# A graph network on one core: the event tiles of layer 1 made as one-hots on VectorE and multiplied in the fifth section, not loaded as byte rows in the last one

## What is computed

```python
def _L1_gnn_ref(x, edge_index, Ws, bs, ln_w, ln_b):
    deg = jnp.zeros((n,), x.dtype).at[dst].add(1.0) + 1.0
    dinv = jax.lax.rsqrt(deg)
    enorm = (dinv[src] * dinv[dst])[:, None]
    self_norm = (dinv * dinv)[:, None]
    h = x
    for l in range(Ws.shape[0]):
        hw = h @ Ws[l]
        agg = jnp.zeros_like(hw).at[dst].add(enorm * hw[src])
        agg = agg + self_norm * hw + bs[l]
        mean = jnp.mean(agg)
        var = jnp.mean(jnp.square(agg - mean))
        hn = ln_w[l] * (agg - mean) * jax.lax.rsqrt(var + EPS) + ln_b[l]
        h = jax.nn.relu(hn)
    return h
```

## Time and profile before

| | us |
|---|---|
| median of 3 runs | 13834.2 |
| lowest and highest | 13832.89, 13850.3 |
| profiled execution, device time | 13845.09 |
| its span, first to last instruction | 13843.3 |
| mean TensorE clock granted, of full speed | 0.697 |

### The profile page before, as it was taken

The page is one execution under the profiler, slowest core; times in us unless marked ns, Lnnn a source line. Parts: engine busy times, 40 slices in busy tenths (PEclk is TensorE's granted clock), DMA queues, the critical chain, the costliest instruction groups (busy, mean ns, idle before and its releaser), DMA issues. The chain is left out here.

```text
span 13843.3 us, 151624 instructions
## 1 busy us (share of the span) xinstructions
PE 7164.9 (52%) x44130; PEld 5810.4 (42%) x44130; DVE 7167.8 (52%) x18509; ACT 4855.9 (35%) x7954; POOL 5410.8 (39%) x5426
## 2 busy tenths in 40 slices
PE   2333333325555555550053000036399999999788
PEld 2222222214454444440032000035255788888676
DVE  5556555634444444442042000158378777777666
ACT  0000000003333333330042000014288777777566
POOL 4555555555555555555714777720300000000111
PEclk6555555556666666665576555568699999999899
DMA  3334333423222222227185000039366888888798
GB/s 125 121 121 133 127 121 120 137 80 66 64 65 63 64 65 63 65 57 40 29 219 147 20 20 20 3 84 223 76 204 204 240 272 254 274 253 271 158 186 173
DMA packets 2774800, 1739.57 MB, mean 126 GB/s; under 512 B 1804710, under 2 KB 2613388, under 8 KB 2773940
## 3 DMA queue, kind: packets, MB, share of 16 engines
q1 hardware_dynamic: 2434740, 1298.35, 36.7%
q10 hardware_dynamic: 165920, 277.72, 5.6%
q0 software_dynamic: 173408, 154.46, 5.0%
HBM read 1065.70 MB, written 506.69 MB: 114 GB/s over the span
## 5 line engine op out<-in xcount | busy, mean ns | idle before, releaser
L838 POOL DMA_INDIRECT records<-RT,IDX x1664 | 1620.3, 974 | 1470.2 <-ACT RT L1598 972.1
L808 POOL DMA_INDIRECT G<-node_table,IDX x1664 | 1605.3, 965 | 1351.7 <-issue 1286.0
L882 POOL DMA_INDIRECT adj<-OH,EA x1664 | 1720.2, 1034 | 639.3 <-issue 639.3
L1276 PE MATMUL PS<-ring_f,terms_r 128*128 128x448 f32 x8232 | 1725.0, 369 | 34.3 <-DVE ring_f L2525 24.9
L1276 PEld LDWEIGHTS PS<-ring_f,terms_r 128*128 128x128 f32 x8232 | 1531.7, 188 | 216.7 <-DVE ring_f L2525 68.5
L2525 DVE CAST ring_f<-raw_f 128x1792 fp32r<-128x1792 uint8 x1323 | 1409.3, 1092 | 395.3 <-DMA raw_f<-adj 245.2
L1762 ACT CAST ring_f<-raw_f 128x1792 fp32r<-128x1792 uint8 x882 | 1465.5, 1691 | 418.4 <-DMA raw_f<-adj 260.3
L1052 PE MATMUL PS<-OH 128*98 128x128 bf16 x3328 | 453.5, 317 | 1806.9 <-remote 855.4
L1052 PEld LDWEIGHTS PS<-OH 128*98 128x98 bf16 x3328 | 365.8, 199 | 1973.4 <-remote 884.3
L2037 DVE TENSOR_TENSOR_SCAN S<-M,S,PS 128x512 f32<-128x512 bf16 x621 | 791.8, 1275 | 748.8 <-issue 517.1
L2030 DVE TENSOR_SCALAR OH<-iota_b,AG 128x128 bf16<-128x128 bf16 (+1 forms) x4480 | 836.0, 269 | 567.5 <-issue 290.6
(11 more groups left out here) (404 smaller groups left out, 14295.4 us busy)
## 6 DMA issues: line engine op xcount, KB each, us to landing
raw_f<-adj SPq DMA_DIRECT2D x2205, 224.0 KB
adj<-Z ACTq DMA_DIRECT2D x105, 1568.0 KB
AG<-adj SPq DMA_DIRECT2D x735, 224.0 KB
G<-records SPq DMA_DIRECT2D x624, 128.0 KB
M<-same_dst SPq DMA_DIRECT2D x416, 128.0 KB
fill_rows<-Z ACTq DMA_DIRECT2D x104, 512.0 KB
runs_l<-R SPq DMA_DIRECT2D x208, 256.0 KB
G<-fill_rows SPq DMA_DIRECT2D x208, 256.0 KB
```

Source lines behind the costliest of these rows:

```text
L808: pool.indirect_dma_start(G[:, i, q * D:(q + 1) * D], None, table, bass.IndirectOffsetOnAxis(ap=IDX[:, i, q:q + 1], axis=0)).then_inc(sem( ...
L838: pool.indirect_dma_start(rec, bass.IndirectOffsetOnAxis(ap=IDX[:, i, q:q + 1], axis=0), RT[:, i, q, :], None).then_inc(sem(f"scattered{i} ...
L882: pool.indirect_dma_start(adj_cells, bass.IndirectOffsetOnAxis(ap=CELL[:, at:at + 1], axis=0), VAL[:, at:at + 1], None).then_inc(sem(f"cel ...
L1276: m = pe.matmul(half_of(x, h)[:, c, :], stat, RINGF[q % NR][:, h * QW + c * HW:h * QW + (c + 1) * HW], start=K == 0, stop=False, skip_grou ...
```

## The change

- The last section no longer has the event tiles: it has 2 row tiles instead of 9, and the ring of layer 1 turns over 686 tiles instead of 735. Four spare tiles fill the last round: they are loaded and turned, PE only counts them.
- `rows_of` keeps the event's destination in `vrow`, less one where there is no event. DVE writes, ahead of the first tile, 98 columns of `dsj` (= `below`), which is `vrow` less 128 times the tile's number.
- In the fifth section (`VPART` = 4, 8 row tiles) DVE makes for each group 7 tiles of one-hots (`virtual_ones`): `iota_f` compared with `dsj`, 128x1792, written as bf16 in two buffers by turns (`VOH`). PE multiplies these seven ahead of the group's eight byte tiles.
- `VIRT_AT` is now the round before the fifth section, and the additions on DVE are placed by tile (`LAST_OF[u] + NR`), no longer by round.
- POOL issues 25 blocks before `virtual_rows` and 14 after it, where it was 35 (after the first 13) and 4.

```diff
-        PART = [list(range(CUTS[c], CUTS[c + 1])) + (list(range(NJ, AB)) if c == NCK - 1 else []) for c in range(NCK)]
+        PART = [list(range(CUTS[c], CUTS[c + 1])) for c in range(NCK)]
+        VPART = 4
...
-        VIRT_AT = LAST_OF[NJ // (2 * GT) * (NCK - 1) - 1] // NR
+        VIRT_AT = LAST_OF[NJ // (2 * GT) * VPART - 1] // NR
+        VOH = [r.bitcast(BF16) for r in REST]
...
+        ONCE = -(-UR * NJ // NR) * NR
+        SPARE = list(range(UR * NJ, ONCE))
...
-            adj_out(NB // 4, NB - 4)
+            adj_out(NB // 4, NB - 14)
             pool.wait_ge(*dve_at("srow_ready"))
             virtual_rows(0, VT)
-            adj_out(NB - 4, NB)
+            adj_out(NB - 14, NB)
...
+                    if c == VPART:
+                        if g == 0:
+                            pe.wait_ge(sem("virt_ready"), 1)
+                        for k in range(NV):
+                            pe.wait_ge(sem("v_ready"), NG2 + g * NV + k + 1)
+                            products(lambda t: VT3[:, t, k * D:(k + 1) * D], VOH[(g * NV + k) % 2], base, x, k == 0, False).then_inc(sem("fm_t"), 1)
...
+            def virtual_ones(g):
+
+                if g:
+                    then(dve.tensor_scalar(dsj, dsj, float(-2 * QW), None, ALU.add))
+                for k in range(NV):
+                    n = g * NV + k
+                    if n >= 2:
+                        dve.wait_ge(sem("fm_t"), NG2 + n - 1)
+                    dve.tensor_tensor(VOH[n % 2].rearrange("p (j c) -> p j c", c=P), rowbc(iota_f[:, :], 2 * GT),
+                                      bc(dsj[:, k * 2 * GT:(k + 1) * 2 * GT], [P, 2 * GT, P]), ALU.is_equal).then_inc(sem("v_ready"), 1)
...
                 for i in BY_DVE:
+                    n = r * NR + i
+                    before = n - (NR - BY_DVE[-1] + BY_DVE[0] if i == BY_DVE[0] else 2)
+                    for u, (c, g) in enumerate(UNIT):
+                        if before < LAST_OF[u] + NR <= n:
+                            if c < NCK - 1:
+                                add_part(u)
+                            else:
+                                scaled(0, g)
+                        if c == VPART and before < FIRST_OF[u] <= n:
+                            virtual_ones(g)
...
-            AFTER = {(LAST_OF[u] + NR) // NR: u for u in range(len(UNIT) - 1)}
-            assert len(AFTER) == len(UNIT) - 1
-            for r in range(NG2 * NK):
+            for k in range(NV):
+                for j in range(2 * GT):
+                    t = dve.tensor_scalar(dsj[:, k * 2 * GT + j:k * 2 * GT + j + 1], vrow[:, k:k + 1], float(-j * P), None, ALU.add)
+            then(t)
+            for r in range(ONCE // NR):
                 if r == VIRT_AT:
                     virtual_terms(0)
                 to_bf16_first(r)
```

More of the change, by code:

```diff
@@ L263, in gnn_kernel @@
         ON_ACT = [K < NJ and n % 2 == 0 for n, (_, K) in enumerate(TILE)]
-        RE = UE * AB
+        ONCE = -(-UR * NJ // NR) * NR
+        SPARE = list(range(UR * NJ, ONCE))
+        RE = ONCE + (UE - UR) * AB
         NW = 7
@@ L417, in gnn_kernel @@
         srj = below[:, 0:NV * 2 * GT]
+        dsj = srj
         assert MID_AT[5] + HALF <= EA_AT + 3 * SLOT and EA_AT + 3 * SLOT + HALF <= EA_END
@@ L727, in _ @@
                         group_end(g, g, g % 2)
+            for n in SPARE:
+                i, r = n % NR, n // NR
+                if i in BY_ACT:
+                    sp.wait_ge(sem("conv_a"), r * NA + i // 2 + 1)
+                else:
+                    sp.wait_ge(sem("conv_d"), r * ND + i // 2 + 1)
+                sp.dma_start(RAW[i], adj[0:P, 0:2 * QW]).then_inc(sem(f"ring_in{i}"), 16)
             sp.wait_ge(sem("conv_a"), A_BASE)
@@ L1334, in by_parts @@
                             pe.wait_ge(sem("conv_d"), r * ND + ND + i // 2 + 1)
[L1335 to L1338, removed]
+                        products(lambda t: TERMS[t][:, K * D:(K + 1) * D], RING[i], base, x, c != VPART and K == CUTS[c],
+                                 c < NCK - 1 and K == PART[c][-1]).then_inc(sem("ring_free"), 1)
                         n += 1
@@ L1341, in by_parts @@
                         own(g, x)
+                pe.wait_ge(sem("group_done"), NG2)
+                for n in SPARE:
+                    i, r = n % NR, n // NR
+                    if i in BY_ACT:
+                        pe.wait_ge(sem("conv_a"), r * NA + NA + i // 2 + 1)
+                    else:
+                        pe.wait_ge(sem("conv_d"), r * ND + ND + i // 2 + 1)
+                    pe.sem_inc(sem("ring_free"), 1)
             projected(0)
@@ L1752, in _ @@
             virtual_terms(0)
-            with act.Fori(VIRT_AT, NG2 * NK) as r:
+            with act.Fori(VIRT_AT, ONCE // NR) as r:
                 to_bf16(0, r)
@@ L2300, in rows_of @@
                 then(dve.tensor_copy(cols[:, :], vrow[:, :]))
+                then(dve.scalar_tensor_tensor(vrow[:, :], row_f[:, :], 0.0, vrow[:, :], ALU.min, ALU.add))
                 dve.sem_inc(sem("dve_at"), 1)
@@ L2406, in to_bf16 @@
                     dve.tensor_copy(RING[i], RAW[i]).then_inc(sem("conv_d"), 1)
+            def virtual_ones(g):
[7 more added lines that the diff above has]
+                                      bc(dsj[:, k * 2 * GT:(k + 1) * 2 * GT], [P, 2 * GT, P]), ALU.is_equal).then_inc(sem("v_ready"), 1)
+            FIRST_OF = [LAST_OF[u] + 1 - len(PART[c]) for u, (c, _) in enumerate(UNIT)]
             def to_bf16_first(r):
                 for i in BY_DVE:
+                    n = r * NR + i
[4 more added lines that the diff above has]
+                                add_part(u)
+                            else:
+                                scaled(0, g)
+                        if c == VPART and before < FIRST_OF[u] <= n:
+                            virtual_ones(g)
                     dve.wait_ge(sem(f"ring_in{i}"), r * 16 + 16)
@@ L2509, in _ @@
                 to_bf16_first(r)
[L2510 to L2514, removed]
             statistics(0, scaled(0, NG2 - 1))
```

4 lines of the change are left out of this document (2 added, 2 removed).

## The result

| | us |
|---|---|
| median of 4 runs after | 13948.0 (13941.47 to 13952.66) |
| median of 4 runs before, same chip | 13836.76 (13832.89 to 13850.3) |
| ratio | 1.0078, 95% interval 1.0061 to 1.0095 |
| profiled execution after: device time, span | 13948.1, 13946.3 |

The change makes the kernel 0.8% slower, 111 us by the medians; 13939 was forecast. The spans differ by 103.0 us, and almost all of it arises in one stretch, from the first cell DMA of the second piece to the statistics of the first layer (the first BATCH_NORM_AGGREGATE). I call it **the stretch**: 10830.6 - 7542.8 = 3287.8 us before, 10932.9 - 7542.3 = 3390.6 us after.

What follows compares the result with a forecast made beforehand. PE was taken to be bound beside the cells to one instruction per cell DMA, 1.40 us apart. Terms 46 + 6 + 34 + 14 + 5 = +105 us on the median 13834.2 gave 13939 us, range 13865 to 14005.

Steps and rivals of the forecast that it cites:

- What bounds: While cells are written, PE gets one instruction per cell DMA, 1.40 us apart; 1664 cell DMAs cost about 2300 us.
- Wherever they stand: Claim that each cell DMA holds PE to one instruction in any place, before or behind the gathers.
- Term 1: 320 cell DMAs moved behind the gathers: 448 us added there, 387 gained ahead, 15 of matmuls done meanwhile; net +46 us.
- the freed stretch: Time before the gathers that the moved cells leave to PE; its work there was put at 61 us at full speed.
- Term 2: 98 small columns ahead of DVE's first tile, 0.067 us each, 6.5 in all, delaying PE's tiles: +6 us (0 to 10).
- Term 3: 49 one-hot tiles at 2.0 us make DVE bound the fifth section, 153 us against PE's 119: +34 us.
- Terms 4 and 5: Last section without event tiles, 38 us against 24: +14 us; spare tiles and a group's scaling in arrears: +5 us.
- PE not held: Rival: moved cells lie beside full-speed products behind the gathers, so 387 us stay gained: 13506 us; chance 0.08.
- The stretch that doesn't close: Rival: projection and chunk stay slow before the gathers for another reason, only loss left: up to 14326 us; chance 0.03.
- Cheap one-hots: Rival: one-hots in the fifth section take about 1.1 us each or are hidden: 13905 us; chance 0.12.
- The clock in the fifth section: Rival: PE's clock falls there as DVE lets it work 78% of the time, up to 85 us more: 14024; chance 0.08.

## Why the prediction was right, point by point

- **What bounds.** PE at one instruction in 1.40 us beside the cells, in both places: right for this chip, as the stretches at 9440 and 9940 show. "Wherever they stand" was right only under a condition that the prediction didn't know: with four memsets between the cells, at 1.49 us a cell, PE does five times the work, and on one of the chips nothing holds it. A backed-up queue would be such a condition, but that is argued, not shown.
- **Term 1, cells moved: 46 forecast, 22 to 37 measured.** The gathers shifted by 395.8 us, not 387, since the freed stretch is worth 448 - 396 = 52 us, not 61: I counted 4 and 9 us for the chunk and the first group from too few rows, and they took 7.8 (8676.1 to 8683.9). Behind the gathers 440.6 us were added (9401.9 to 10048.9 against 9797.7 to 10004.1), not 448. By the stretch the cells alone cost 37 us in the kernel before and 22 in the changed one; by the totals the 37 don't show. Right in sign by the traces, too large in size.
- **Term 2, small columns: 6 forecast, 1 to 16 measured.** Terms 1 and 2 together cost 38 us, where 52 were forecast. How they share it depends on the order in which they are put in: 37 and 1, or 22 and 16. The columns took 12.6 us, not 6.5, as only part of them came at 0.067 us each; between others DVE was idle. They fall into the few microseconds before PE slows down, in which PE did 73 matmuls before (9798 to 9811): the kernel with the cells' split alone has done 396 matmuls when full speed returns, the changed one 311, 85 x 0.095 = 8 us.
- **Term 3, one-hots: 34 forecast, 33 measured.** 2.019 us each, the section 152.4 us against 153, PE waiting for them, and 33 us gone when DVE is spared them. The Trainium skill (VectorE: DVE Perf Modes, the section on the TRN2 errata) has a formula that gives an estimate of 2.02 us for a 1792-column f32 `tensor_tensor`; the trace agrees.
- **Terms 4 and 5, last section and spare tiles: 19 forecast, 32 measured.** This is the term that was most mis-sized. The section took 56 us, not 38. I priced a unit by DVE's work (4.9 us) and gave 0.5 us for "a little waiting since SP holds the next loads". That waiting is most of the price: DVE waits five times in the seven groups for a load, 3.4 to 5.6 us each, 22.7 in all, and issuing the next loads ahead gives 18 to 20 us back. The granted clock in that section was 0.79 on the mean, between the levels of 1.2 and 2.4 GHz (0.50 and 1.00), with PE busy for 34 of 56 us; the earlier trace rows have 1.00 with PE busy for 95%. What the clock costs there was not measured.
- **The sum** came out at 105 for 103 by luck: terms 1 and 2 were 14 too high, term 3 one, and terms 4 and 5 were 13 too low. The kernel with the cells put back says the same by its stretch: all terms but the first cost 81 us, and 59 were forecast. By its total it is only 50 us over the kernel before on its chip.
- **The rivals.** PE not held: excluded on the chip of the forecast, and what happens on the fast one, though there it brings no gain as POOL is then the bound. The stretch that doesn't close: a group of 6.83 us from 8697 on excludes it. Cheap one-hots: 2.019 us. The clock in the fifth section: 1.00.

## What to carry to other kernels

When one engine is slow beside another's DMAs in a steady beat, compare how fast those DMAs can be issued with how fast they are issued. If the issuing engine is being held back, it is worth trying a few small instructions between its DMAs: here POOL went from 1.39 to 1.49 us a cell and the kernel took 6% less time, though why is not shown. Work moved out of a section takes its cover along: a wait for loads that PE's tiles had hidden becomes the price of what is left, so look at what the queue's own engine waits for there before a section is made short. And a change measured on one chip is a change where that chip's bound is: 1.0078 on one was 1.0007 on another.

## What the runs showed of the hardware that I had not expected

- Indirect DMAs of single bytes (128 a DMA), which POOL can issue at 1.27 us each, were issued at 1.39 us on the mean in the kernel before, and PE did one instruction in 1.40 us beside them, while all DMAs together moved 20 GB/s. With four memsets between them it was 98 GB/s at 1.49 us a cell. No run shows which resource is held. The Trainium skill (Runtime: NRT & Kernel Launch, Instruction fetch mechanics) has instructions fetched by a DMA queue of their own; that this queue is held back like the loads is a guess that nobody tested, and it would still have to explain why PE's instructions come singly, 1.40 us apart.
- Chips differ in this. The kernel before took 10202 us on one and 13824 to 13856 on the others (medians). The changed kernel's trace on that one differs from the kernel before's on a slower one where POOL issues indirect DMAs: a cell comes every 1.27 us (79 in 100 us) instead of 1.39, a gather of the first stage (the group on the page whose output is G) every 1.34 instead of 1.78. No run shows why.
- Memsets of one column on 32 partitions, in four groups of partitions in turn, took POOL 0.14 us each (1.13 for eight). On all 128 partitions one alone took 0.12, and four in a row only 0.20 together.
